# The shared expert's down product of a vision block, computed straight into rows of tokens instead of columns

## The chip, the cores and the metric

The kernel runs on one core of one Trainium2 chip. The metric is the device time of one execution in microseconds (us). A time is given as the median of several executions; a profile is one execution more, with its own time.

## The reference, cut to what matters

64 images give 38 tokens each (36 patches and two class tokens), 2432 tokens of 256 channels. One block follows: a gated linear attention on the normalised tokens, then a mixture of 32 experts with a shared expert. The part that the change touches is the shared expert:

```python
def _swiglu(x, gw, uw, dw):
    return jax.nn.silu(x @ gw) * (x @ uw) @ dw
...
shared_out = _swiglu(x, shared_gate_w, shared_up_w, shared_down_w)
...
return (shared_out + routed_out).reshape(b, s, h)
```

Here x has 256 channels and the hidden layer 512. The result is added to the residual, and each token's row is then added to the output of the one expert that the router picked for it.

## The kernel before, in words

**Phase one, groups.** The images go through in G = 8 groups of 8 images, so GT = 304 tokens a group. A group passes four stages: embedding (e), front (f: first layer norm, up product, convolution), attention (a), and mixture (m: second layer norm, router, shared expert). In each step of the program four different groups stand in the four stages. What follows what on each engine is written out by hand in one function `step` for each engine; semaphores with counts tie the engines together. The last three groups, called `near` (group 5), `next_last` (group 6) and `last` (group 7), leave the pipeline in three blocks that are written out in full behind the loop, with fewer stages in each.

**Layouts.** Products that contract over channels want channels on the partitions ("columns": 128 channels by 304 tokens). Layer norms, residual and stores want tokens on the partitions ("rows": three tiles of 114, 114 and 76 tokens, which `height(j)` and `columns(j)` give, with 256 channels). `to_rows` turns columns into rows by transposes on TensorE.

**The shared expert of a group.** For each of four chunks k of 128 hidden channels `gate_up(m, k)` makes gate and up in the banks mb[0] and mb[1]; ScalarE makes `silu_g` of the first, VectorE multiplies it with the second into `act_t[:, k, :]` (128 hidden channels by 304 tokens). `shared_down` then makes the product in columns: a 128x128 piece of the weights `sd_w` lies still, the 304 columns of `act_t` move. ScalarE copies both halves from the banks to `ffn_t`, six transposes of `ffn_rows` bring them back to the banks as rows, and `base_of` on VectorE adds the residual `h2` and writes `base_rows`, which SyncE stores and GpSimd scatters to the expert's zone in memory.

A product of f32 operands is executed as two passes, each with its own load of the weights: the 8 matmuls of 304 columns are 16 passes in the trace. Transposes are one pass each.

**Around it.** In a step of the pipeline TensorE runs `gate_up(m, 3)`, `up(f, 7)`, `shared_down(m)`, `embed(e, 0)`, `ffn_rows(m)`, `heads_t(a)`, `embed(e, 1)`, `down(a)`. `embed(e, 0)` waits until `silu_z` of the front stage has been read out of its bank. In the written-out blocks `shared_down` comes in two halves, placed between other work. `stream` is a matmul whose result nobody reads.

**Phase two, experts.** 37 slots of 128 tokens each (32 and five more for overfull experts). Each slot loads its expert's weights (1.5 MB), its token rows `xg` from the zones, and computes the expert; TensorE passes straight from the last `ffn_rows` to the transposes of the first slot's `xg`, ScalarE makes `x_hi` and VectorE `x_lo` of them, on which the first product waits.

Of the kernel before, what the change touches and what calls it, by code (L numbers as in the profile page):

```python
# [13 lines left out]
D = 256  # L14
# [9 lines left out]
GT = GS * S  # L24
# [21 lines left out]
def height(j):  # L46

    return SHORT if j == NT - 1 else R
# [10 lines left out]
def groups_phase(nc, block, patches, w_lin, pos, cols, w_up, conv, chan, wq, wk, wv, wvt, w_gates, b_gates,  # L59
# [6 lines left out]
    with ExitStack() as ctx:  # L66
        def sb(name, shape, dt=f32):
            return ctx.enter_context(nc.sbuf_tensor(name, shape, dt))

        def sem(name):  # L70
            return ctx.enter_context(nc.semaphore(name))
# [91 lines left out]
        act_t = sb("act_t", [128, KI, GT])  # L163
        ffn_t = sb("ffn_t", [128, KD, GT])
        base_rows = sort.base_rows
# [127 lines left out]
        s_act = sem("s_act")  # L293
        s_sd_mm = sem("s_sd_mm")
        s_ffn = sem("s_ffn")
        s_ft_mm = sem("s_ft_mm")
# [197 lines left out]
        def _(act):  # L494
# [9 lines left out]
            def copy(dst, src):  # L504
                return act.activation(dst, src, ACT.Copy)  # L505
# [140 lines left out]

            def ffn_t_of(m, halves=range(KD)):
                for c in halves:
                    act.wait_ge(s_sd_mm, KD * m.n + c + 1)
                    copy(ffn_t[:, c, :], mb[c][:, 0:GT]).then_inc(s_ffn, 1)  # L650

            def step(e, f, a, m):
# [43 lines left out]
                if f and f.n == 1:  # L696
                    x_act_of(f, 0)
                    x_act_of(f, 1)
                if m: ffn_t_of(m)
                if a: att_t_of(a)  # L700
# [40 lines left out]
            x_act_of(f, 1)  # L741
            ffn_t_of(m, (0,))

# [10 lines left out]
            v_of(a, 2)  # L754
            ffn_t_of(near, (1,))
            decay(a, 0)
# [11 lines left out]
            score_rows(m)  # L768
            ffn_t_of(m, (0,))
            att_t_of(a, (0,))  # L770
            ffn_t_of(m, (1,))

            def last_group(split):
                m = last
                xn2_t_of(m)
                split(0, 0)
                tanh_score(m)
                silu_g_of(m, 0)
                score_rows(m)
                silu_g_of(m, 1)  # L780
                split(0, 1)
                silu_g_of(m, 2)
                split(1, 0)
                silu_g_of(m, 3)
                split(1, 1)
                ffn_t_of(m)

# [519 lines left out]
        def _(pe):  # L1307
# [259 lines left out]

            def shared_down(m, halves=range(KD)):
                pe.wait_ge(s_act, KI * m.n + KI)
                for c in halves:  # L1570
                    for k in range(KI):
                        last = pe.matmul(mb[c][:, 0:GT], sd_w[:, k, c * 128:(c + 1) * 128], act_t[:, k, :],  # L1572
                                         start=(k == 0), stop=(k == KI - 1))
                    last.then_inc(s_sd_mm, 1)

            def ffn_rows(m):
                pe.wait_ge(s_ffn, KD * m.n + KD)
                to_rows(mb, ffn_t, s_ft_mm)

            def step(e, f, a, m):  # L1580
# [46 lines left out]
                if f: up(f, 7)  # L1627
                if m: shared_down(m)
                if e: embed(e, 0)
                if m: ffn_rows(m)  # L1630
                if a: heads_t(a)
# [48 lines left out]
            att_rows(a)  # L1680
            shared_down(m, (0,))

# [5 lines left out]
            v_of(a, 0)  # L1688
            shared_down(near, (1,))
            v_of(a, 1)  # L1690
# [3 lines left out]
            gates_t(a)  # L1694
            ffn_rows(near)
            tops_t(a)
# [13 lines left out]
            heads_t(a)  # L1710
            shared_down(m, (0,))
            down(a)
            att_rows(a)
            shared_down(m, (1,))
            ffn_rows(m)

# [11 lines left out]
            gate_up(m, 3)  # L1728
            shared_down(m)
            sort.slot_table(pe)  # L1730
            ffn_rows(m)

# [640 lines left out]
```

## Time and profile before

| | before |
|---|---|
| median of 3 runs | 653.28 us (651.33 to 653.66) |
| the profiled execution | 654.7 us |
| its span, first to last instruction | 652.9 us |
| mean granted TensorE clock | 0.988 of full |
| TensorE busy | 607.6 us, 93% |
| VectorE busy | 429.5 us, 66% |
| ScalarE busy | 375.2 us, 57% |

The span is what the trace shows; the time holds 1.8 us more for start and end. In the views an instruction's row begins with its start from the beginning of the span. "PE" is TensorE's matmuls, "PEld" its loads of weights, which overlap them, "DVE" VectorE, "ACT" ScalarE, "POOL" GpSimd and "SPq" the queue of SyncE. A matmul's duration holds its way through the array, so it is longer than the distance to the next one; what a pass costs in a row of passes is that distance.

### The profile page before, as it was taken

Reading aid. Unit: us, or ns where it says so; the run is one execution under the profiler, and the core shown is the slowest. Engines: PE = TensorE matmul, PEld = TensorE weight load, DVE = VectorE, ACT = ScalarE, POOL = GpSimd, SP = SyncE. Lnnn points to the kernel's source line nnn. Section 1 sums busy time; section 2 is a strip of 40 time slices with the busy share of each in tenths; the row PEclk is TensorE's granted clock in tenths of the full one; section 3 lists DMA queues with packets and bytes.
Section 4 is the critical chain, followed back from the end, with each engine's and each line's share of the span. In section 5 each row is a group of like instructions: output and inputs, shape, how many; then the busy total and the mean of one; then the engine's idle time right before and its main releaser. Section 6 shows DMA issues by size and latency. Waiting matters only on the chain.

```text
span 652.9 us, 10636 instructions
## 1 busy us (share of the span) xinstructions
PE 607.6 (93%) x3615; PEld 510.1 (78%) x3615; DVE 429.5 (66%) x1338; ACT 375.2 (57%) x839; POOL 197.4 (30%) x226
## 2 busy tenths in 40 slices
PE   4899899999998998999999998988999999999995
PEld 3688778878878878878878977766788888888884
DVE  1644785865856865866765866675876777776672
ACT  1328668449439529539538758243666666666661
POOL 5100110231232133133033233353256662232451
PEclk9999899999999999999998999899999999999999
DMA  8339410030030030030010011185999999999960
GB/s 291 132 85 369 122 56 1 20 94 21 20 95 21 20 94 21 19 95 21 8 51 20 2 37 37 35 303 169 392 391 378 379 348 350 373 369 404 343 214 23
DMA packets 44597, 101.56 MB, mean 156 GB/s; under 512 B 9295, under 2 KB 30589, under 8 KB 39672
## 3 DMA queue, kind: packets, MB, share of 16 engines
q1 hardware_dynamic: 35280, 89.07, 38.1%
q0 software_dynamic: 7696, 8.49, 4.7%
q10 hardware_dynamic: 1560, 3.23, 1.5%
q8 instruction: 32, 0.52, 0.4%
q14 instruction: 29, 0.24, 0.1%
HBM read 80.17 MB, written 23.32 MB: 159 GB/s over the span
## 4 chain that ended last, share of the span: by engine, by line
PE 71%; ACT 14%; DVE 8%; issue 2%; POOL 1%; DMA 1%; SPq 0%; DVEq 0%; ACTq 0%; POOLq 0%
PE bank L2253 16%; PE bank L1390 11%; PE bank L2272 9%; PE bank L1355 8%; PE bank L1512 4%; PE bank L1490 3%; PE bank L1455 3%; PE bank L2261 2%; PE bank L1416 2%; PE bank L1572 2%; PE bank L1364 2%; ACT v L505 2%; ACT hst L581 2%; ACT L596 1%; ACT L592 1%
## 5 line engine op out<-in xcount | busy, mean ns | idle before, releaser
L456 POOL TENSOR_TENSOR rstd_h<-var_h,minus_half 114x4 f32<-114x4 f32 (+1 forms) x24 | 24.3, 1014 | 173.3 <-DVE var_h L999 173.3
L2077 POOL DMA_INDIRECT out<-rows,bg x32 | 37.6, 1175 | 82.4 <-DVE rows L2143 81.1
L1355 PE MATMUL bank<-patch,lin_w 128*128 128x288 f32 x192 | 52.6, 428 | 8.7 <-DMA col_t<-cols 7.9
L2253 PE MATMUL bank<-w_hi,x_hi 128*128 128x512 f32 x148 | 56.5, 463 | 2.7 <-DVE x_lo L2155 2.7
L1355 PEld LDWEIGHTS bank<-patch,lin_w 128*128 128x128 f32 x192 | 37.4, 201 | 20.6 <-DMA col_t<-cols 7.9
L898 DVE SCALAR_TENSOR_TENSOR y<-xm,conv_t,y 128x296 f32<-128x296 f32 (+2 forms) x96 | 43.7, 512 | 6.2 <-ACT xm L505 6.2
L2253 PE MATMUL bank<-w_lo,x_hi 128*128 128x512 f32 x148 | 46.3, 394 | 0.0
L2253 PE MATMUL bank<-w_hi,x_lo 128*128 128x512 f32 x148 | 46.2, 393 | 0.0
L2179 DVE TENSOR_TENSOR act_e<-silu_e,bank 128x512 f32<-128x512 f32 x37 | 25.5, 688 | 31.0 <-PE bank L2253 30.3
L2149 DVE TENSOR_TENSOR w_lo<-wts,w_hi 128x1024 fp32r<-128x1024 f32 x36 | 43.1, 1217 | 0.5 <-ACT w_hi L2201 0.5
L2228 ACT ACTIVATE silu_e<-bank 128x512 f32<-128x512 f32 x37 | 22.1, 598 | 35.2 <-PE bank L2253 35.2
L1390 PE MATMUL bank<-xn_hi,up_hi 128*128 128x304 f32 x128 | 33.7, 346 | 6.0 <-ACT xm L505 4.9
L1841 POOL DMA_INDIRECT b_zone_dram<-base_rows,spot x24 | 31.1, 1295 | 26.9 <-DVE base_rows L1125 20.9
L505 ACT ACTIVATE att_t<-bank 128x304 f32<-128x304 f32 x15 | 6.3, 423 | 54.1 <-PE bank L1512 53.4
L2201 ACT ACTIVATE w_hi<-wts 128x1024 fp32r<-128x1024 f32 x36 | 36.8, 1049 | 0.0
L1841 POOL DMA_INDIRECT x_zone_dram<-xs_rows,spot x24 | 30.2, 1259 | 21.1 <-DVE spot L1103 9.0
L2196 ACT ACTIVATE x_hi<-bank 128x256 fp32r<-128x256 f32 x37 | 14.2, 383 | 38.9 <-PE bank L2242 28.1
L2143 DVE SCALAR_TENSOR_TENSOR rows<-bank,bg 128x256 f32<-128x256 f32 x37 | 15.7, 424 | 31.2 <-PE bank L2272 19.3
L1572 PE MATMUL bank<-act_t,sd_w 128*128 128x304 f32 x128 | 35.0, 424 | 1.2 <-DVE act_t L1117 1.2
L1390 PE MATMUL bank<-xn_hi,sgu_hi 128*128 128x304 f32 x128 | 31.6, 329 | 3.4 <-DVE act_t L1117 2.9
L1512 PE MATMUL bank<-hst,down_w 128*128 128x304 f32 x128 | 34.1, 420 | 0.1
L2272 PE MATMUL bank<-wts_down,act_et 128*128 128x256 f32 x144 | 34.1, 379 | 0.0
(261 smaller groups left out, 1658.8 us busy)
## 6 DMA issues: line engine op xcount, KB each, us to landing
wts<-w_exp SPq DMA_DIRECT2D x18, 1024.0 KB
x_act<-w_exp SPq DMA_DIRECT2D x10, 1024.0 KB
silu_z<-w_exp SPq DMA_DIRECT2D x9, 1024.0 KB
wts_down<-w_exp SPq DMA_DIRECT2D x18, 512.0 KB
patch<-patches SPq DMA_DIRECT2D x8, 864.0 KB, 6.0
down_w<-w_exp SPq DMA_DIRECT2D x10, 512.0 KB
lin_w<-w_exp SPq DMA_DIRECT2D x9, 512.0 KB
b_zone_dram<-act_t SPq DMA_DIRECT2D x1, 4160.0 KB, 28.4
```

Source lines behind the costliest of these rows:

```text
L898: dve.scalar_tensor_tensor(y[:, k, :, lag:], xm[:, f.p, k, :, 0:S - lag], w, y[:, k, :, lag:], ALU.mult, ALU.add).then_inc(s_conv, 1)
L1355: last = pe.matmul(fb[c][:, 0:GS * N], lin_w[:, k, c * 128:(c + 1) * 128], patch[:, k, :], start=(k == 0), stop=(k == KF - 1))
L1390: last = pe.matmul(dst, weights[w][:, c, at:at + 128], x[part][:, c, :], start=(n == 0), stop=(n == 3 * KD - 1))
L1512: last = pe.matmul(ab[c][:, 0:GT], down_w[:, k, c * 128:(c + 1) * 128], hst[:, k, :], start=(k == 0), stop=(k == KI - 1))
L1572: last = pe.matmul(mb[c][:, 0:GT], sd_w[:, k, c * 128:(c + 1) * 128], act_t[:, k, :], start=(k == 0), stop=(k == KI - 1))
L1841: pool.indirect_dma_start(zone, bass.IndirectOffsetOnAxis(ap=self.spot[0:n, t:t + 1], axis=0), rows[0:n, j, :], None, bounds_check=E * SLO ...
L2077: pool.indirect_dma_start(out, bass.IndirectOffsetOnAxis(ap=rows_at, axis=0), rows[:, k % 4, :], None, bounds_check=T - 1, oob_is_err=Fals ...
L2149: dve.tensor_tensor(w_lo[:, k % 2, u, :], wts[k % 4][:, u * KD * I:(u + 1) * KD * I], w_hi[:, k % 2, u, :].bitcast(f32), ALU.subtract).the ...
L2179: dve.tensor_tensor(act_e[:, e, :], silu_e[:, e, :], banks[3 + 2 * e][:, :], ALU.mult).then_inc(s_ae, 1)
L2201: act.activation(w_hi[:, k % 2, u, :], wts[k % 4][:, u * KD * I:(u + 1) * KD * I], ACT.Copy).then_inc(s_w_hi, 1)
L2253: last = pe.matmul(banks[2 + 2 * e + u][:, :], x[:, e, c * SLOT:(c + 1) * SLOT], w[:, e, u, c * I:(c + 1) * I], start=(n == 0), stop=(n == ...
L2272: last = pe.matmul(banks[6 + k % 2][:, 0:D], act_et[:, k % 2, c, :], wts_down[k % 4][:, c * D:(c + 1) * D], start=(c == 0), stop=(c == KI ...
```

## The change

The product is turned round. A tile of tokens of `act_t` (128 hidden channels by 114 or 76 tokens) lies still, and the 256 columns of `sd_w[:, k, :]` move. The result has tokens on the partitions, so `base_of` reads it from the banks as it is. `ffn_t`, the two copies of ScalarE and the six transposes are gone. Tiles 0 and 1 go to the two halves of mb[0], tile 2 to mb[1]. The first three products of tile 0 wait only for their own chunk of `act_t`, all others for the last one.

```diff
-        ffn_t = sb("ffn_t", [128, KD, GT])
...
-            def ffn_t_of(m, halves=range(KD)):
-                for c in halves:
-                    act.wait_ge(s_sd_mm, KD * m.n + c + 1)
-                    copy(ffn_t[:, c, :], mb[c][:, 0:GT]).then_inc(s_ffn, 1)
...
-            def shared_down(m, halves=range(KD)):
-                pe.wait_ge(s_act, KI * m.n + KI)
-                for c in halves:
+            def ffn_rows(m, tiles=range(NT)):
+                pe.wait_ge(s_sg, KI * m.n + KI)
+                for j in tiles:
                     for k in range(KI):
-                        last = pe.matmul(mb[c][:, 0:GT], sd_w[:, k, c * 128:(c + 1) * 128], act_t[:, k, :],
-                                         start=(k == 0), stop=(k == KI - 1))
-                    last.then_inc(s_sd_mm, 1)
-
-            def ffn_rows(m):
-                pe.wait_ge(s_ffn, KD * m.n + KD)
-                to_rows(mb, ffn_t, s_ft_mm)
+                        pe.wait_ge(s_act, KI * m.n + (k + 1 if j == 0 and k < KI - 1 else KI))
+                        last = pe.matmul(mb[j // 2][0:height(j), (j % 2) * D:(j % 2 + 1) * D], act_t[:, k, columns(j)],
+                                         sd_w[:, k, :], start=(k == 0), stop=(k == KI - 1))
+                    if j > 0:
+                        last.then_inc(s_ft_mm, 1)
...
                 if f: up(f, 7)
-                if m: shared_down(m)
+                if m: ffn_rows(m)
                 if e: embed(e, 0)
-                if m: ffn_rows(m)
                 if a: heads_t(a)
...
             att_rows(a)
-            shared_down(m, (0,))
+            ffn_rows(m, (0, 1))
...
             v_of(a, 0)
-            shared_down(near, (1,))
+            ffn_rows(near, (2,))
             v_of(a, 1)
...
             gates_t(a)
-            ffn_rows(near)
             tops_t(a)
...
             heads_t(a)
-            shared_down(m, (0,))
+            ffn_rows(m, (0, 1))
             down(a)
             att_rows(a)
-            shared_down(m, (1,))
-            ffn_rows(m)
+            ffn_rows(m, (2,))
...
             gate_up(m, 3)
-            shared_down(m)
+            ffn_rows(m)
             sort.slot_table(pe)
-            ffn_rows(m)
```

Three places of TensorE's order show what moved. A row counts matmuls as the program issues them (an f32 one is two passes), the shape is that of the result. First a step of the pipeline, from the last product of the front stage to the attention's down product. Before:

```order
622 L1390 MATMUL bank<-xn_lo,up_hi 128x304 x2
623 L1572 MATMUL bank<-act_t,sd_w 128x304 x8
624 L1355 MATMUL bank<-patch,lin_w 128x288 x6
625 L1364 MATMUL bank<-ident,ffn_t 114x128 x4
626 L1364 MATMUL bank<-ident,ffn_t 76x128 x2
627 L1501 MATMUL bank<-ident,o 128x114 x8
628 L1501 MATMUL bank<-ident,o 128x76 x4
```

And now:

```order
618 L1376 MATMUL bank<-xn_lo,up_hi 128x304 x2
619 L1559 MATMUL bank<-sd_w,act_t 114x256 x8
620 L1559 MATMUL bank<-sd_w,act_t 76x256 x4
621 L1341 MATMUL bank<-patch,lin_w 128x288 x6
622 L1487 MATMUL bank<-ident,o 128x114 x8
623 L1487 MATMUL bank<-ident,o 128x76 x4
```

Twelve matmuls of 256 columns stand ahead of the embedding where there were eight of 304, and nothing of the shared expert stands behind it any more. Second the block of group 6, where its shared expert meets the attention of group 7 (`o` is transposed by `heads_t`, `hst` read by `down`, `att_t` by `att_rows`; `ident` and `sd_w` with 128x512 is the filler). Before:

```order
789 L1501 MATMUL bank<-ident,o 128x114 x8
790 L1501 MATMUL bank<-ident,o 128x76 x4
791 L1572 MATMUL bank<-act_t,sd_w 128x304 x4
792 L1512 MATMUL bank<-hst,down_w 128x304 x8
793 L1364 MATMUL bank<-ident,att_t 114x128 x4
794 L1364 MATMUL bank<-ident,att_t 76x128 x2
795 L1572 MATMUL bank<-act_t,sd_w 128x304 x4
796 L1364 MATMUL bank<-ident,ffn_t 114x128 x4
797 L1364 MATMUL bank<-ident,ffn_t 76x128 x2
798 L1347 MATMUL bank<-sd_w,ident 128x512
799 L1381 MATMUL bank<-ident,xn 128x114 x2
```

And now:

```order
782 L1487 MATMUL bank<-ident,o 128x114 x8
783 L1487 MATMUL bank<-ident,o 128x76 x4
784 L1559 MATMUL bank<-sd_w,act_t 114x256 x8
785 L1498 MATMUL bank<-hst,down_w 128x304 x8
786 L1350 MATMUL bank<-ident,att_t 114x128 x4
787 L1350 MATMUL bank<-ident,att_t 76x128 x2
788 L1559 MATMUL bank<-sd_w,act_t 76x256 x4
789 L1333 MATMUL bank<-sd_w,ident 128x512
790 L1367 MATMUL bank<-ident,xn 128x114 x2
```

Ahead of the attention's down product four matmuls have become eight, behind it four matmuls and six transposes have become four matmuls. Third the end of phase one: the last group's shared expert, the small product of `slot_table` (from `slot_e`), and the first transposes and products of phase two. Before:

```order
838 L1390 MATMUL bank<-xn_lo,sgu_hi 128x304 x2
839 L1572 MATMUL bank<-act_t,sd_w 128x304 x8
840 L1910 MATMUL bank<-ident,slot_e 1x114
841 L1364 MATMUL bank<-ident,ffn_t 114x128 x4
842 L1364 MATMUL bank<-ident,ffn_t 76x128 x2
843 L2234 UNCONDITIONAL_BRANCH
844 L2242 MATMUL bank<-ident,xg 128x128 x2
```

And now:

```order
829 L1376 MATMUL bank<-xn_lo,sgu_hi 128x304 x2
830 L1559 MATMUL bank<-sd_w,act_t 114x256 x8
831 L1559 MATMUL bank<-sd_w,act_t 76x256 x4
832 L1890 MATMUL bank<-ident,slot_e 1x114
833 L2214 UNCONDITIONAL_BRANCH
834 L2222 MATMUL bank<-ident,xg 128x128 x2
```

The transposes between the slot table and the first slot are gone.

## Rows read from the trace of the kernel before

**Rows 1.** Page: busy us, share and instructions of the engines.

```profile
PE 607.6 (93%) x3615; PEld 510.1 (78%) x3615; DVE 429.5 (66%) x1338; ACT 375.2 (57%) x839; POOL 197.4 (30%) x226
```

**Rows 2.** Timeline of TensorE in one step of the pipeline: start, us, instruction, idle before.

```profile
222.54 4.32 PE L1572 MATMUL bank<-act_t,sd_w 128*128 128x304 f32 x16
227.02 3.15 PE L1355 MATMUL bank<-patch,lin_w 128*128 128x288 f32 x12 [0.16 <-ACT silu_z L544]
230.00 0.82 PE L1364 MATMUL bank<-ident,ffn_t 128*114 128x128 f32 x6
230.66 1.21 PE L1501 MATMUL bank<-ident,o 114*128 114x114 f32 x12
```

**Rows 3.** The chain that ended last: start, us, pieces of 304 and 256 columns.

```profile
234.83 4.09 PE bank L1512 x16
...
483.46 1.73 PE bank L2272 x8
```

**Rows 4.** Groups of instructions: busy us, mean ns of one, idle before.

```profile
L2272 PEld LDWEIGHTS bank<-wts_down,act_et 128*128 128x128 f32 x144 | 26.0, 190 | 2.9
```

**Rows 5.** Timeline of ScalarE in that step.

```profile
226.44 0.43 ACT L544 ACTIVATE silu_z<-bank 128x304 f32<-128x304 f32 x1
```

**Rows 6.** Timeline of TensorE between group 5's last products and group 7's decay.

```profile
380.72 0.82 PE L1364 MATMUL bank<-ident,att_t 128*114 128x128 f32 x6
382.10 2.31 PE L1572 MATMUL bank<-act_t,sd_w 128*128 128x304 f32 x8 [0.56 <-DVE act_t L1117]
384.25 2.21 PE L1416 MATMUL bank<-x_act,score_w 128*128 128x304 f32 x8
387.03 2.50 PE L1455 MATMUL bank<-q_t,x_act 128*114 128x122 f32 x24 [0.58 <-ACT q_t L566]
...
394.60 0.28 PE L1461 MATMUL bank<-logf,tri 114*114 114x12 f32 x2
```

**Rows 7.** Timeline of VectorE there.

```profile
394.15 0.17 DVE L924 SCALAR_TENSOR_TENSOR logf<-gl,fln 114x12 f32<-114x12 f32 x1 [2.38 <-ACT fln L596]
```

**Rows 8.** Timelines of TensorE, VectorE and GpSimd in group 6's block.

```profile
415.17 2.25 PE L1572 MATMUL bank<-act_t,sd_w 128*128 128x304 f32 x8
417.48 4.33 PE L1512 MATMUL bank<-hst,down_w 128*128 128x304 f32 x16
422.38 0.87 PE L1364 MATMUL bank<-ident,att_t 128*114 128x128 f32 x6 [0.57 <-DVE att_t L1029]
...
425.70 0.89 POOL L450 TENSOR_TENSOR rstd<-rstd,minus_half 114x3 f32<-114x3 f32 x1
...
426.60 1.02 DVE L1125 TENSOR_TENSOR base_rows<-bank,h 114x512 f32<-114x512 f32 x2 [1.31 <-PE bank L1364]
427.54 1.06 DVE L1054 TENSOR_SCALAR xn<-h,mv,rstd 114x256 f32<-114x256 f32 x3
```

**Rows 9.** Timeline of all engines where phase two begins.

```profile
441.22 4.36 PE L1572 MATMUL bank<-act_t,sd_w 128*128 128x304 f32 x16 [0.64 <-DVE act_t L1117]
...
444.14 0.82 SPq L2006 DMA_DIRECT2D xg<-x_zone_dram  x2
...
446.80 0.38 PE L2242 MATMUL bank<-ident,xg 128*128 128x128 f32 x2
446.88 1.02 DVE L1125 TENSOR_TENSOR base_rows<-bank,h 114x512 f32<-114x512 f32 x2 [1.82 <-PE bank L1364]
447.22 0.38 ACT L2196 ACTIVATE x_hi<-bank 128x256 fp32r<-128x256 f32 x1 [1.18 <-PE bank L2242]
...
447.96 0.40 DVE L2155 TENSOR_TENSOR x_lo<-bank,x_hi 128x256 fp32r<-128x256 f32 x1
448.42 0.73 PE L2253 MATMUL bank<-w_hi,x_hi 128*128 128x512 f32 x2 [1.24 <-DVE x_lo L2155]
```

**Rows 10.** Sums by stretch: us, busy of the engines, granted clock, DMA.

```profile
404.50:407.90 3.40, 1.24 (x10) 0.98 (x8) 3.19 (x23) 0.89 (x4) 1.33 (x2) 1.00 0.01 4
...
407.97:411.30 3.33, 3.33 (x15) 3.29 (x16) 2.76 (x19) 1.63 (x6) 1.37 (x2) 0.50 0.02 5
```

More of the change, by code:

```diff
@@ L293, in groups_phase @@
         s_act = sem("s_act")
-        s_sd_mm = sem("s_sd_mm")
-        s_ffn = sem("s_ffn")
         s_ft_mm = sem("s_ft_mm")
@@ L698, in step @@
                     x_act_of(f, 1)
-                if m: ffn_t_of(m)
                 if a: att_t_of(a)
@@ L741, in _ @@
             x_act_of(f, 1)
-            ffn_t_of(m, (0,))
             a, m = last, next_last
@@ L754, in _ @@
             v_of(a, 2)
-            ffn_t_of(near, (1,))
             decay(a, 0)
@@ L768, in _ @@
             score_rows(m)
-            ffn_t_of(m, (0,))
             att_t_of(a, (0,))
-            ffn_t_of(m, (1,))
             def last_group(split):
@@ L785, in last_group @@
                 split(1, 1)
-                ffn_t_of(m)
             sort.last_act = last_group
```

## The prediction, made before the changed kernel ran

> **What bounds the kernel now.** I read the page first: TensorE is busy for 93% of the span, no other engine above 66% [rows 1]. So an edit counts by what it does to TensorE's sequence of work, and by the few places where TensorE waits. The timeline of TensorE shows those. In the five steps of the pipeline in which the shared expert of groups 0 to 4 runs, the product, the embedding's first half, the six transposes of `ffn_t` and the head transposes follow each other with one short wait, for `silu_z` on ScalarE [rows 2]. In the written-out blocks of groups 5, 6 and 7 fewer stages run beside each other, and waits decide more [rows 6, 8, 9]. Behind the last group TensorE starts the experts at once, and the first product there waits for a chain over ScalarE and VectorE [rows 9].
>
> **The price of a pass.** In the chain 16 passes of 304 columns take 4.09 us and 8 passes of 256 columns take 1.73 us [rows 3]: 0.256 and 0.216 us a pass. Six transposes take 0.66 us, the distance from 230.00 to 230.66 in [rows 2], while their row lasts 0.82 us: a row's modelled end outlasts its turn by 0.16 us. I use that below: work that waited could have started by the shown idle time plus 0.16 us earlier.
>
> The new product has the stationary operand 114 or 76 wide, which no row shows together with 256 columns. Its bounds are the two prices above: 0.216 as in the experts' down product, which also moves 256 columns of f32 weights past stationary activations, and at most the 0.256 of the wider passes. I take 0.216, since columns and operands are the same. The load of weights takes 0.190 us there [rows 4], under the 0.216 of the pass beside it, and shows no cost.
>
> One rule of the Trainium skill speaks against this (TensorE: Matmul & The Clock Gate, Part 3, The mechanism): a load of weights overlaps running matmuls only where it addresses other row groups of the array. All loads here address the same ones. By it each pass would pay for its load; by [rows 3, 4] it does not, for 8 passes with 8 loads of 0.190 us took 1.73 us in all. The sum goes by the rows.
>
> **The work itself.** Removed for a group: 16 passes (16 x 0.256 = 4.10) and 6 transposes (0.66), 4.76 us of TensorE. Added: 12 matmuls, 24 passes, 24 x 0.216 = 5.18 us. TensorE does 0.42 us more for each group, 8 x 0.42 = 3.4 us in all. ScalarE loses two copies a group and VectorE nothing. The question is how much of the 3.4 us comes back out of waits.
>
> **Groups 0 to 4, in the pipeline: +0.04 us each, +0.2.** The product starts at 222.54, the embedding at 227.02 instead of 226.70 (idle 0.16 and 0.16), because `silu_z` ends at 226.87 [rows 2, 5]. From 222.54 to the head transposes at 230.66 are 8.12 us. Now: 5.18 for the passes and 0.06 to get going end at 227.78, behind `silu_z`, so nothing waits; the embedding needs 12 passes, 230.00 - 227.02 = 2.98 with a restart or 2.92 without; the head transposes start at 230.70. The wait has paid for the longer product. If that cover were gone, each step would cost 0.36. The copies taken from ScalarE and the earlier `base_rows` on VectorE free no one there: the steps behind wait for TensorE's own results.
>
> **Group 5: +0.4.** The first half waited for the last chunk of `act_t`: started at 382.10, could have at 382.10 - 0.56 - 0.16 = 381.38 [rows 6]. Now the first three products of tile 0 need only the earlier chunks, 6 passes, 1.3 us, and cover the wait. 16 passes end at 381.38 + 0.06 + 3.46 = 384.9, where `q_of` started at 384.25: 0.6 later, and ScalarE's copies of q, for which the scores wait 0.58 us, move along. Tile 2 then takes 8 x 0.216 = 1.73 instead of 8 x 0.256 = 2.05, 0.3 back, of which what counts is where TensorE meets the forget gates: `logf` was ready at 394.32 and its sum started at 394.60 [rows 6, 7]. With `logf` 0.6 later, 394.92 plus some hundredths, the sum starts at about 395.0: +0.4. The transposes that are gone behind it stood in time in which TensorE waited for the scan of the gates on VectorE, so their 0.66 us return nothing.
>
> **Group 6: +0.25.** Two tiles (3.46 and 0.06) stand ahead of `down` where 8 passes did: it starts at 415.17 + 3.52 = 418.7 instead of 417.48, 1.2 later, and so does everything up to `att_rows` (422.38) and the second layer norm's statistics of group 7. SyncE's first loads of expert weights move by the same; their first reader is ScalarE behind its copy of group 7's second norm, which stands further down this same chain, so nothing new waits for them. But before, VectorE stood with `base_rows` (426.60 to 427.62) between the statistics and `xn`, just after the 1/std was ready at 425.70 + 0.89 = 426.59 [rows 8]. Tile 2 now starts behind `att_rows`, at 422.38 + 1.15 + 0.71 = 424.25, is done at 426.0, and VectorE does `base_rows` while GpSimd makes the 1/std, which is ready at about 427.75. `xn` starts at 427.8 instead of 427.54. So 1.2 us late becomes 0.25.
>
> **Group 7: -1.0.** Here the product waited 0.64 us for `act_t` and could have started at 441.22 - 0.64 - 0.16 = 440.42 [rows 9]. Three products of tile 0 cover that wait again: 440.42 + 0.06 + 5.18 = 445.66, the slot table is two short passes, 0.2 like two transposes, so the first transposes of `xg` could run at 445.9 instead of 446.80. Their rows were asked for at 444.14 and were there by 446.8; when exactly, no row says. I take 446.2. Then VectorE: before, `base_rows` and the table held it to 447.96 although `x_hi` was ready at 447.22 + 0.38 = 447.60; now `base_rows` is nearly done by then. `x_lo` starts about 0.75 us behind the transposes, at 446.95, the first expert product at 447.4 instead of 448.42: -1.0. Bounds: transposes at 445.9 give -1.35, at 446.7 they give -0.4.
>
> **Sum.** 0.2 + 0.4 + 0.25 - 1.0 = -0.15 us. The profiled execution took 654.7 us, 1.4 above the median of the runs; the difference applies to both. 653.28 - 0.15 = **653.1 us**. Phase two is unchanged: a slot every 5.3 us on TensorE. A measurement of this kernel tells a change of about 0.5%, 3.3 us, from none.
>
> **Rivals.**
> - The work shows in full: no wait gives anything back, because the operands of tile 0 or `silu_z` come later than I read. All 3.4 us of added passes stay: 656.7. It is slower than before by the 0.5% bound only if practically nothing is returned, or if a pass costs more than 0.216: 192 new passes at 0.256 add 7.7 us to my sum, 660.8. It decides from 0.234 us a pass (3.4 / 192 = 0.018 over). For it: the operand's width has no row. Against: 0.256 belongs to more columns. Chance 0.08.
> - Loads of weights are not hidden behind passes of 256 columns. The mechanism in this kernel: each of the 192 passes pays its load of 0.190 [rows 4] as well, +36 us, 690. This is what the rule named above would do here. Against it stand the same 8 passes in 1.73 us [rows 3]. Chance 0.01.
> - The clock. After a stretch in which TensorE was busy for 1.24 of 3.40 us the clock was granted at half for 3.3 us (0.50, that is 1.2 GHz), which costs about 1.65 us [rows 10]. Group 6's block now has a pause of about 1.2 us ahead of the transposes of `xn`, for the transposes of `ffn_t` are gone and the filler runs earlier; and every other wait shifts a little. One such stretch more: 654.8. Chance 0.14. One less, since the last blocks have moved: 651.5. Chance 0.13.
> - Group 6's delay is not returned, because VectorE's `base_rows` still stands before `xn` (tile 2 late): 654.1. Chance 0.08.
> - The change helps more: the earlier start of phase two and ScalarE's free time take more than 3.3 us out. For it I find no wait of that size behind the places changed. Chance 0.04.
>
> **How the numbers follow.** My forecast has the remaining 0.52, with its own range of 652.3 to 653.9 from the bounds of group 7 and the spread of the terms. Slower by over 0.5%: the first two rivals, 0.09. Faster by over 0.5%: the last rival, and 0.01 for two clock stretches less, 0.05. Within 0.5%: the rest, 0.86. The median before itself came from runs 2.3 us apart, so the range takes in one clock stretch either way: 651.2 to 655.4.
>
> **What would show each step.** A distance of 0.216 us between the new passes; from the start of the product to the head transposes about 8.16 us in the pipeline, without a wait ahead of the embedding; in group 5 the scores 0.6 us later relative to `att_rows`; in group 6 `down` 3.5 us behind the product's start and `base_rows` ahead of the ready 1/std; in group 7 no idle time before the product and some 7.0 us from its start to the first expert product (7.2 before, and from a start that was 0.8 later). I would be wrong if passes are dearer, if the many waits on `act_t`, one for each matmul, hold up the loads of weights, or if half-clock stretches come or go.

## The result, and the profile after

| | before | after |
|---|---|---|
| median, both kernels on the same chips | 653.28 us (13 runs) | 656.81 us (13 runs) |
| ratio, 95% interval | | 1.0062 [1.0038, 1.0086] |
| the profiled execution | 654.7 us | 660.08 us |
| its span | 652.9 us | 658.3 us |
| mean granted clock | 0.988 | 0.979 |

The change makes the kernel 3.5 us slower. The forecast was 653.1 us, no change. One execution far above the rest (699.68 us, of e3 below) and one of the kernel before (3382.77 us, beside e1 to e4) are left out of the ratios. The page of after, busy us and share of each engine (against [rows 1]):

```profile
PE 614.0 (93%) x3631; PEld 518.0 (79%) x3631; DVE 429.6 (65%) x1338; ACT 370.0 (56%) x823; POOL 197.6 (30%) x226
```

TensorE is busy for 6.4 us more, of which the added passes explain 3.4. The timeline of TensorE in the step of [rows 2]:

```profile
222.83 5.34 PE L1559 MATMUL bank<-sd_w,act_t 128*114 128x256 f32 x24
228.01 3.07 PE L1341 MATMUL bank<-patch,lin_w 128*128 128x288 f32 x12
230.92 1.21 PE L1487 MATMUL bank<-ident,o 114*128 114x114 f32 x12
```

The 24 passes take 228.01 - 222.83 = 5.18 us, 0.216 each, no wait stands ahead of the embedding, and from the product to the head transposes it is 8.09 us where it was 8.12. The same holds from step to step: from group 0's product (start at 121.76 us, before 121.45) to group 4's (323.90, before 323.66) it is 202.14 us, before 202.21. The pipeline costs nothing.

Group 5's block, TensorE from `att_rows` on (against [rows 6]):

```profile
384.15 0.82 PE L1350 MATMUL bank<-ident,att_t 128*114 128x128 f32 x6
384.81 3.62 PE L1559 MATMUL bank<-sd_w,act_t 128*114 128x256 f32 x16
388.26 2.21 PE L1402 MATMUL bank<-x_act,score_w 128*128 128x304 f32 x8
...
398.38 0.37 PE L1447 MATMUL bank<-logf,tri 114*114 114x12 f32 x2
399.26 0.28 PE L1453 MATMUL bank<-ident,a_gate 114*114 114x114 f32 x1 [0.51 <-DVE fsum L919]
400.23 0.31 PE L1457 MATMUL bank<-ident,top_gate 114*114 114x114 f32 x1 [0.69 <-DVE top_gate L924]
400.79 0.40 PE L1465 MATMUL bank<-mask_bf,ident_bf 114*114 114x456 bf16 x1 [0.24 <-DVE top_parts L930]
...
404.86 2.06 PE L1333 MATMUL bank<-sd_w,ident 128*128 128x512 f32 x2
406.71 1.06 PE L1476 MATMUL bank<-v,cw 114*114 114x128 f32 x4
```

The block is reached 3.4 us later than before, since the clock was at half from 353.9 us on for longer; that differs from execution to execution in both kernels (below). Inside the block, `att_rows` to `logf`'s sum is 14.23 us, before 13.88. At the gates TensorE now waits 0.51, 0.69 and 0.24 us. Before, the six transposes of `ffn_t` stood in between, and it waited 0.51 and 0.38:

```profile
395.39 0.29 PE L1467 MATMUL bank<-ident,a_gate 114*114 114x114 f32 x1 [0.51 <-DVE fsum L933]
396.06 0.87 PE L1364 MATMUL bank<-ident,ffn_t 128*114 128x128 f32 x6 [0.38 <-ACT ffn_t L505]
396.76 0.26 PE L1471 MATMUL bank<-ident,top_gate 114*114 114x114 f32 x1
396.92 0.40 PE L1479 MATMUL bank<-mask_bf,ident_bf 114*114 114x456 bf16 x1
```

And the filler (L1333) takes 2.06 us instead of 1.1. The windows say why. A row gives the stretch and its length, then the busy time (and the number of instructions) of TensorE, its loads, VectorE, ScalarE and GpSimd, then TensorE's granted clock and the DMA's share and GB/s:

```profile
395.00:398.20 3.20, 3.20 (x28) 2.89 (x26) 0.82 (x4) 3.14 (x6) 0.00 (x0) 1.00 0.00 0
398.20:401.60 3.40, 1.96 (x14) 1.35 (x13) 2.84 (x12) 2.81 (x6) 0.00 (x0) 1.00 0.01 2
401.70:408.50 6.80, 6.80 (x33) 5.74 (x32) 3.93 (x19) 5.35 (x19) 3.51 (x3) 0.50 0.31 89
```

TensorE was busy for 1.96 of 3.40 us at the gates, and then the clock was granted at 0.50, 1.2 GHz, for 6.8 us. In the kernel before the same place had 1.00:

```profile
394.70:398.00 3.30, 2.41 (x21) 2.01 (x19) 2.81 (x11) 2.88 (x7) 0.00 (x0) 1.00 0.00 0
398.00:401.40 3.40, 3.40 (x31) 2.91 (x30) 2.72 (x15) 3.36 (x16) 2.24 (x2) 1.00 0.26 73
```

These stretches aren't cut at the same instructions. Cut alike, as the 3.40 us from 14.05 us behind the start of `att_rows`, the busy time of TensorE at the gates is 1.96 us in after and was 2.51 before. The profile of before has its own 3.3 us at half clock further on, from 407.9 us [rows 10]; after has none there.

Group 6 (against [rows 8]) behaves as forecast: `down` stands 3.49 us behind the product, and `base_rows` lies ahead of the ready 1/std.

```profile
421.02 3.65 PE L1559 MATMUL bank<-sd_w,act_t 128*114 128x256 f32 x16
424.51 4.26 PE L1498 MATMUL bank<-hst,down_w 128*128 128x304 f32 x16
...
432.17 1.02 DVE L1111 TENSOR_TENSOR base_rows<-bank,h 114x512 f32<-114x512 f32 x2
...
432.65 0.89 POOL L447 TENSOR_TENSOR rstd<-rstd,minus_half 114x3 f32<-114x3 f32 x1
...
433.57 1.05 DVE L1040 TENSOR_SCALAR xn<-h,mv,rstd 114x256 f32<-114x256 f32 x3 [0.39 <-POOL rstd L447]
```

Group 7 (against [rows 9]), all engines:

```profile
446.16 1.45 POOL L1821 DMA_INDIRECT x_zone_dram<-xs_rows,spot  x1 [0.30 <-issue]
...
451.08 0.82 SPq L1986 DMA_DIRECT2D xg<-x_zone_dram  x2
...
453.11 0.44 PE L2222 MATMUL bank<-ident,xg 128*128 128x128 f32 x2 [1.02 <-DMA xg<-x_zone_dram]
...
454.48 0.73 PE L2233 MATMUL bank<-w_hi,x_hi 128*128 128x512 f32 x2 [0.93 <-DVE x_lo L2135]
```

TensorE is free at 452.1 and waits 1.02 us for the rows of `xg`. SyncE asked for them 4.92 us behind the start of the last scatter into the zone; before it was 444.14 - 440.13 = 4.01, with this scatter:

```profile
440.13 1.45 POOL L1841 DMA_INDIRECT x_zone_dram<-xs_rows,spot  x1 [0.30 <-issue]
```

### The profile page after: what moved, and what is told of

It is laid out like the page before. It is cut to its first block, busy times and chain, and to the rows that moved or that the text cites. A ratio compares the mean times of both kernels' runs of the same rounds, so it can differ in the third digit from the quotient of the medians.

```text
span 658.3 us, 10662 instructions
## 1 busy us (share of the span) xinstructions
PE 614.0 (93%) x3631; PEld 518.0 (79%) x3631; DVE 429.6 (65%) x1338; ACT 370.0 (56%) x823; POOL 197.6 (30%) x226
## 4 chain that ended last, share of the span: by engine, by line
PE 76%; ACT 12%; DVE 7%; issue 2%; POOL 1%; DMA 1%; SPq 0%; DVEq 0%; POOLq 0%
PE bank L2233 16%; PE bank L1376 12%; PE bank L2252 9%; PE bank L1341 8%; PE bank L1559 5%; PE bank L1498 5%; PE bank L1476 3%; PE bank L1441 3%; PE bank L2241 2%; PE bank L1402 2%; ACT hst L578 2%; ACT v L502 1%; PE bank L1350 1%; PE bank L1487 1%; PE bank L1413 1%
## 5 line engine op out<-in xcount | busy, mean ns | idle before, releaser
L1559 PE MATMUL bank<-sd_w,act_t 128*114 128x256 f32 (+1 forms) x192 | 43.1, 379 | 0.0
L1559 PEld LDWEIGHTS bank<-sd_w,act_t 128*114 128x114 f32 (+1 forms) x192 | 31.7, 168 | 8.2
```

The source lines that it names most:

```text
L1559: last = pe.matmul(mb[j // 2][0:height(j), (j % 2) * D:(j % 2 + 1) * D], act_t[:, k, columns(j)], sd_w[:, k, :], start=(k == 0), stop=(k = ...
```

## The experiments

Ratios are to the kernel before on the same chip, with 95% intervals, of 12 or 13 executions of each kernel and 23 to 35 of before. A "stretch" is time at half clock in the profiled execution; "at the gates" is the place at 401.7 us in after. Stretches elsewhere differ from profile to profile of one and the same kernel. Both kernels have one at about 353 us in most profiles (3.4 or 10.2 us, sometimes none), and mostly short ones at 33 and 74 us. One of 3.4 us at about 408 us is in the profiles of before, e5 and e9, and not in those of e1 and e3. Short ones where phase two begins are told of at the end. The table of landmarks further down begins behind the stretches at 33, 74 and 353 us. One profile shows one execution; so the mean granted clock, which every execution has, is compared as well.

**1. Which part.** Both kernels again, the new product in groups 0 to 4 alone, and in groups 5 to 7 alone. The line of e3 (in e4 the pipeline keeps the old lines and the three blocks have the new ones):

```diff
                 if f: up(f, 7)
-                if m: shared_down(m)
+                if m: ffn_direct(m)
                 if e: embed(e, 0)
-                if m: ffn_rows(m)
                 if a: heads_t(a)
```

> The kernel before, unchanged, as a control and for the granted clock of every run. Two theories of the 3.5 us are at stake. Clock theory: the new passes cost what was forecast and waits return them, but TensorE is granted the half clock for longer in the blocks written out behind the pipeline. Then here runs at a lower mean clock are the longer ones, by about half of the time at half clock: 0.001 of mean clock is worth about 0.65 us, and the mean clock lies near 0.988. Work theory: the 3.4 us of added passes stay in the time whatever the clock does; then before and after differ at equal clock.

> The changed kernel, unchanged, on the same chip. Clock theory: about 3.5 us slower in the median, at a mean clock lower by about 0.005, and equal to before at equal clock to within 1 us; the profile's stretches at half clock add up to more than those of before, around 353 and 401 us. Work theory: slower by 3.4 us also at equal clock.

> The new product only in the five steps of the pipeline (groups 0 to 4); groups 5, 6 and 7 keep columns, copies and transposes. Clock theory: same as before to within 0.5 us, for the steps of the pipeline measured 0.03 us shorter each in the trace of the change and have no half clock. Work theory: 5 x 0.42 = 2.1 us slower.

> The new product only in the written-out blocks of groups 5, 6 and 7; the pipeline is as before. Clock theory: all of the loss is here, 3 to 4 us slower than before, with a mean clock as low as that of the change. Work theory: 3 x 0.42 = 1.3 us slower.

| | median us | ratio | stretch at the gates |
|---|---|---|---|
| e1 before again | 650.12 | 0.9979 [0.9956, 1.0002] | none |
| e2 after again | 654.82 | 1.0063 [1.0033, 1.0093] | 6.8 us |
| e3 groups 0 to 4 | 652.62 | 1.0024 [0.9996, 1.0052] | none |
| e4 groups 5 to 7 | 654.98 | 1.0053 [1.0023, 1.0083] | 6.8 us |

The loss repeats and comes with the written-out blocks. The theory that the added work simply stays wanted 2.1 us in e3 and 1.3 in e4; the ratios give 1.6 and 3.5 us. The profile of e4, its slowest execution (661.3 us), has a second stretch, behind the wait of 1.26 us ahead of group 6's `xn`:

```profile
432.60:436.00 3.40, 2.08 (x8) 0.90 (x8) 2.18 (x7) 0.74 (x2) 2.79 (x3) 1.00 0.89 360
436.10:442.80 6.70, 6.10 (x29) 5.96 (x30) 2.19 (x18) 2.88 (x6) 1.37 (x2) 0.50 1.03 380
```

That is the place that the prediction feared. It came in one of the eight profiles with that order there (after, e2, e4, e5, e6, e13, e16, e18).

**2. Which group, or a filler.** e5 keeps columns in group 5; e6 and e7 are the changed kernel with fillers, e8 is the kernel before with its transposes moved.

```diff
             gates_t(a)
+            pe.wait_ge(s_v, NT * a.n + 1)
+            stream(ab[0], sd_w, 1)
             tops_t(a)
...
             m = last
-            stream(ab[1], sd_w, 1)
+            stream(ab[1], sd_w, 2)
```

The last two lines are in e7 only. e8:

```diff
             gates_t(a)
-            ffn_rows(near)
             tops_t(a)
+            ffn_rows(near)
```

> The changed kernel with group 5 alone left in columns, with its copies and its six transposes between the gates' transpose and the tops' transpose. Theory gates: the transposes stood in a wait of TensorE (it now idles 0.69 and 0.24 us there) and kept the activity of that stretch up; without them the clock is halved for 6.8 us from about 401 us. Then this kernel has no 6.8 us stretch there and loses at most 1 to 2 us to before. Rival, the pause of 1.25 us in group 6's block or the experts' start costs it: then it is as slow as the change, 3.5 us.

> The changed kernel with one dummy matmul of 512 columns (two passes, 0.86 us, result unread) in the wait ahead of the tops' transpose in group 5's block; more work, nothing shared with the product itself. Theory gates: no half clock from 401 us, about 2 to 3 us faster than the change, although TensorE does 0.86 us more. Rival theories (the work of the passes, or the pause in group 6's block): same as the change or up to 0.2 us slower.

> As the last, and the filler ahead of the transposes of xn of group 7 doubled, which covers most of the pause of 1.25 us in group 6's block. If that pause also halves the clock in some executions (one profile of the kernel with the change in the blocks alone had a stretch at 436 us), this is faster by up to 1 us than the filler at the gates alone; if not, the same.

> The kernel before with one edit: group 5's six transposes stand behind the tops' transpose instead of ahead of it, so TensorE idles in the wait for the scan, as in the changed kernel. The decay starts 0.4 us later at most. Theory gates: the half clock comes from about 400 us on and this kernel is 2 to 3.5 us slower than before, at a lower mean clock, without any new product. Rivals: at most 0.4 us slower.

| | median us | ratio | stretch at the gates |
|---|---|---|---|
| e5 group 5 in columns | 654.11 | 1.0028 [1.0003, 1.0053] | none |
| e6 filler at the gates | 653.12 | 1.0016 [1.0000, 1.0031] | none |
| e7 and ahead of `xn` | 652.76 | 1.0022 [0.9998, 1.0046] | none |
| e8 before, moved | 651.64 | 1.0007 [0.9984, 1.0030] | none |

More work on TensorE made the kernel faster: e6 does 0.87 us more than after, and its ratio is 1.0016 where after's is 1.0062 and e2's 1.0063, with intervals that don't meet. e7's second filler adds nothing that can be measured. e8 missed its forecast of 2 to 3.5 us: the transposes stand behind `top_gate`'s wait there, and no stretch follows, so to have the wait uncovered isn't enough. e5 has no stretch at the gates and is still 1.8 us slower than before, by an interval that just excludes 1; its profile has three others, at 354, 408 and 449 us. What is left there, and why, is open.

**3. A better version?** e9 spreads the new product's tiles (in group 5 behind `att_rows`, behind the first v and behind `gates_t`; in group 6 tile 0 ahead of `down`, 1 and 2 behind `att_rows`), leaves out the filler ahead of group 7's `xn` and moves VectorE's `base_rows` behind `xn_lo`. e10 is the kernel before without its filler behind `decay`. e11 is e9, e12 the kernel before, each with a filler at 351 us:

```diff
+            pe.wait_ge(s_v, NT * a.n + 1)
+            stream(ab[0], sd_w, 1)
             f_sums(a)
             gates_t(a)
             up(f, 0)
```

> The changed kernel with the tiles of the product placed otherwise in two blocks: group 5's tile 0 ahead of q, tile 1 behind the first values, tile 2 in the wait behind the gates' transpose; group 6's tile 0 ahead of the attention's down product, tiles 1 and 2 behind its rows, in place of the filler, with VectorE's base_rows behind xn_lo of group 7. Amount theory (what counts for the clock is how much TensorE does in the stretch around the gates, and placement costs what the sum says): no half clock at 400 us; the decay of group 7 0.6 us earlier than before, the transposes of xn 0.9 us earlier; 1.5 to 2 us faster than before, 4 to 5 faster than the change. Rival, the new product itself lowers the clock wherever it stands: still 2 us or more slower than before.

> The kernel before with one edit: without the dummy matmul of 512 columns behind group 7's decay, in a stretch in which TensorE then waits for the weighted scores. It takes 0.86 us of TensorE's activity out of the same stretch from which the change took 0.66 us of transposes. Amount theory: half clock from 401 us in most executions, as in the change, 2 to 3 us slower than before. Rival, the clock follows the new product or its place and not the amount: same as before within 0.5 us.

> As the spread kernel, with one dummy matmul of 512 columns ahead of the sum of the forget gates in group 6's attention, about 351 us, in the 0.36 us wait there (it also delays that sum by up to 0.4 us). At about 353.5 us the clock falls in both kernels, for 3.4 us in some profiles and 10.2 us in others. If the amount of activity decides, it falls less often here: 1 to 2 us faster than the spread kernel in the median, and without executions at 655 us and over.

> The kernel before with the same filler at 351 us and nothing else. Amount theory: 1 to 2 us faster than before in the median, for the same reason. It tells whether a gain of the last kernel belongs to the change or could be had without it.

e9: 652.26 us, 1.0017 [0.9987, 1.0047]. e10: 651.85, 1.0005 [0.9979, 1.0032], and no stretch at the gates. e11: 650.44, 0.9970 [0.9941, 0.9998]. e12: 649.82, 0.9963 [0.9939, 0.9987]. The gain of e11 is that of the filler, for e12 has it without the change. e9 missed its forecast of 1.5 to 2 us faster than before. On the path the spread tiles do gain: the first expert product comes 65.20 us behind `att_rows` in e11, 66.43 in e12. But e11's profile has a 3.4 us stretch where phase two begins, and from that product to the end it takes 204.7 us, e12 202.7.

e10 missed its forecast too, and it doesn't test what it was meant to. In before, the filler that it leaves out starts at 399.48 us, 18.8 us behind `att_rows`; in after the clock falls about 17.5 us behind them, ahead of that filler. In the 3.40 us at the gates TensorE is busy for 2.51 us in e10, as in before; it is the next 3.40 us that have 3.06 instead of 3.40. A stretch of 3.4 us comes later in e10's profile, at 412.4 us.

In e12 the place where both kernels mostly ran at half clock reads

```profile
350.00:360.20 10.20, 9.31 (x77) 8.36 (x78) 6.74 (x31) 9.76 (x27) 2.89 (x2) 1.00 0.12 32
```

against this row of after:

```profile
353.95:364.10 10.15, 10.15 (x51) 9.98 (x51) 4.79 (x23) 7.31 (x20) 0.00 (x0) 0.50 0.01 4
```

**4. The six transposes themselves.** e13 is the changed kernel with six transposes that nobody reads, at their old place:

```diff
             gates_t(a)
+            pe.wait_ge(s_v, NT * a.n + 1)
+            for j in range(NT):
+                for c in range(KD):
+                    pe.transpose(ab[0][0:height(j), c * 128:(c + 1) * 128], sd_w[:, c, 0:height(j)], ident[:])
             tops_t(a)
```

e14 is the kernel before with the new product in group 5 alone, e15 the same for group 7 alone:

```diff
-            shared_down(m)
+            ffn_direct(m)
             sort.slot_table(pe)
-            ffn_rows(m)
```

e16 is the changed kernel with the fillers of e6 and of e12.

> The changed kernel with six transposes that nobody reads (0.66 us of TensorE) at the place where group 5's transposes were. If the six transposes kept TensorE active enough there: no stretch at half clock near 401 us, granted clock in the medians up from 0.983-0.987 to about 0.990, ratio to before 1.001 to 1.003. If only more work than that (the filler's 0.8 us) does it, or if what they were waiting for mattered: the stretch stays and the ratio stays 1.006.

> The kernel before with the new product in group 5 alone. If group 5's missing transposes bring the half clock near 401 us: a stretch of about 6.8 us there, ratio 1.004 to 1.006, nearly the whole loss. If the stretch needs the other groups too: no such stretch, 1.000 to 1.001 from the 0.4 us of longer product.

> The kernel before with the new product in group 7 alone. By the prediction: first expert product 1.0 us earlier counted from the start of the product's wait, ratio 0.9985. By the reading of the trace (rows of xg land about 2 us after SyncE asks for them, and TensorE waits for them): from group 7's gate products to the first expert product -0.2 to +0.5 us, ratio 1.000 to 1.001, no clock stretch at 401 us.

> The changed kernel with both fillers, at the gates of group 5's block and at 351 us. If the loss is the half clock plus about 1 us of longer order: clock 0.993 to 0.997, about 651 us, ratio to before 0.998, some 1 us above the kernel before with its filler (649.8, 0.9963). If the product itself still costs its 3.4 us: 653, 1.002. If it costs nothing at an even clock: 649.8.

| | median us | lowest us | ratio |
|---|---|---|---|
| e13 dead transposes | 652.82 | 650.68 | 1.0018 [0.9992, 1.0045] |
| e14 group 5 alone | 654.38 | 653.03 | 1.0063 [1.0032, 1.0094] |
| e15 group 7 alone | 652.16 | 649.29 | 0.9993 [0.9959, 1.0027] |
| e16 two fillers | 653.03 | 650.84 | 1.0006 [0.9983, 1.0029] |

e14 changes nothing but group 5 and has the whole loss; e13 leaves the change as it is, adds work without use, and takes most of the loss away. The intervals of the two ratios overlap a little, and e13's profile happens to have no stretch at all, not at 33, 74 or 353 us either, so the profile alone wouldn't do. The clock of the single executions settles it: of the 49 executions of after, e2, e4 and e14 none has a mean granted clock above 0.992; e13 has four of 12 at 0.995 to 0.999, e6 four of 12 at 0.995 to 0.997, and of the 128 of the kernel before beside e1 to e18, 44 lie above 0.992, the highest at 0.998. e16 missed its 651 us by 2: with both fillers the change is as fast as before, no faster. TensorE at the gates in e14:

```profile
393.58 0.28 PE L1465 MATMUL bank<-ident,a_gate 114*114 114x114 f32 x1 [0.51 <-DVE fsum L931]
394.55 0.31 PE L1469 MATMUL bank<-ident,top_gate 114*114 114x114 f32 x1 [0.69 <-DVE top_gate L936]
395.10 0.40 PE L1477 MATMUL bank<-mask_bf,ident_bf 114*114 114x456 bf16 x1 [0.25 <-DVE top_parts L942]
```

and in e13:

```profile
393.24 0.28 PE L1453 MATMUL bank<-ident,a_gate 114*114 114x114 f32 x1 [0.51 <-DVE fsum L919]
393.36 0.82 PE L1681 MATMUL bank<-ident,sd_w 128*114 128x128 f32 x6
394.21 0.31 PE L1457 MATMUL bank<-ident,top_gate 114*114 114x114 f32 x1
394.77 0.40 PE L1465 MATMUL bank<-mask_bf,ident_bf 114*114 114x456 bf16 x1 [0.24 <-DVE top_parts L930]
```

`a_gate` to the first `mask_bf` is 1.52 us in e14 and 1.53 in e13; before it was 396.92 - 395.39 = 1.53. The dead transposes cost no time on the path and fill the pause. The windows of e14:

```profile
392.80:396.40 3.60, 2.16 (x16) 1.70 (x17) 2.97 (x11) 3.01 (x8) 0.00 (x0) 1.00 0.00 0
396.55:403.30 6.75, 6.75 (x31) 5.69 (x31) 3.61 (x19) 5.62 (x17) 3.52 (x3) 0.50 0.31 90
```

and of e13:

```profile
392.00:395.40 3.40, 2.62 (x22) 1.94 (x19) 2.70 (x11) 2.97 (x6) 0.00 (x0) 1.00 0.01 2
395.50:402.00 6.50, 6.50 (x56) 5.99 (x55) 5.42 (x30) 6.37 (x20) 3.65 (x3) 1.00 0.32 90
```

Cut alike, as the 3.40 us from 14.05 us behind the start of `att_rows`, TensorE is busy at the gates for 1.96 us in after, e4 and e14, 1.97 in e2 and 2.62 in e13. So the amount and the clock go together in these; what in the work counts, and how much of it is needed, the runs don't tell.

**5. Group 7's missing microsecond.** e17 is e15 with e12's filler, e18 has the new product in group 6 as well.

```diff
-            shared_down(m, (0,))
+            ffn_direct(m, (0, 1))
             down(a)
             att_rows(a)
-            shared_down(m, (1,))
-            ffn_rows(m)
+            ffn_direct(m, (2,))
```

> The kernel before with the new product in group 7 alone and the filler at 351 us. If group 7's 0.8 us and the filler's 2.5 us add up: about 649.0, ratio 0.995, clock 0.993 or more, 17.3 us from group 7's router to the first expert product. If group 7's part is lost again once the filler is there: 649.8, 0.996, 18.1 us.

> The same with the new product in group 6 as well. If group 6's earlier rows bring the late landing of group 7's scatter: from the last scatter into x_zone_dram to SyncE's request for xg 4.7 to 5.3 us instead of 4.1, and 17.9 to 18.5 us from the router to the first expert product; ratio 0.996. If the late landing comes from the pipeline or from group 5: 4.1 us, 17.3 us, ratio 0.995. In both no half clock near 401 us, for group 5 keeps its transposes.

e17: 651.66 us, 0.9990 [0.9967, 1.0013]; it was meant to be the fastest version and isn't measurably so. e18: 652.71, 1.0017 [0.9996, 1.0037]. The traces are clearer. SyncE and GpSimd in e17, the last scatter and what follows it:

```profile
425.11 0.36 SPq L1833 DMA_DIRECT2D wts<-w_exp  x1
...
441.00 0.82 SPq L2016 DMA_DIRECT2D xg<-x_zone_dram  x2
```

```profile
436.80 1.45 POOL L1851 DMA_INDIRECT x_zone_dram<-xs_rows,spot  x1 [0.30 <-issue]
```

and in e18:

```profile
426.10 1.56 SPq L1830 DMA_DIRECT2D wts<-w_exp  x1
...
443.09 0.82 SPq L2013 DMA_DIRECT2D xg<-x_zone_dram  x2
```

```profile
438.18 1.45 POOL L1848 DMA_INDIRECT x_zone_dram<-xs_rows,spot  x1 [0.30 <-issue]
```

From scatter to request 4.20 us in e17 and 4.91 in e18. Group 6's new form is what delays it. Their times don't show group 7's gain, and hardly can: from the first expert product to the end, where the kernels are alike, the profiles without a stretch there differ by up to 1.9 us (202.6 in e14, 204.5 in before).

**The landmarks**, starts on TensorE read from the timelines, in us from the transposes of group 5's `att_rows`. The stretches at 33, 74 and 353 us lie ahead of them.

| start of | e1 before | after | e13 | e15 | e18 |
|---|---|---|---|---|---|
| `logf` sum | 13.88 | 14.23 | 14.23 | 13.88 | 13.87 |
| decay's first `v,cw` | 19.69 | 22.56 | 20.14 | 19.69 | 19.68 |
| `heads_t` of group 7 | 32.14 | 35.82 | 32.53 | 32.15 | 32.13 |
| router of group 7 | 48.35 | 52.22 | 48.93 | 48.37 | 48.53 |
| first `xg` transpose | 64.82 | 68.96 | 65.75 | 64.30 | 65.23 |
| first expert product | 66.44 | 70.33 | 67.12 | 65.67 | 66.60 |

## Why the prediction was wrong

**The price of a pass and the work itself: right.** 0.216 us a pass, with loads that cost nothing. Both rivals on it fall: the passes aren't dearer than 0.216, and 24 loads ahead of 24 passes took 5.18 us in all. The first rival's other half, that no wait gives anything back, named 656.7 us, and 656.81 was measured; that is a coincidence, for e6, e7, e13 and e16 do all the added work and more and lose 0.4 to 1.4 us.

**Groups 0 to 4: right.** Forecast +0.04 us a step, the trace has 8.09 for 8.12, -0.03, and -0.07 over four steps. e3's 1.0024 has an interval that holds 1; it shows no loss, and excludes none below 3.4 us.

**Group 5: +0.4 forecast, +0.35 at `logf`'s sum and +0.45 at the decay in e13.** The sum was right. The sentence behind it was not: "The transposes that are gone behind it stood in time in which TensorE waited for the scan of the gates on VectorE, so their 0.66 us return nothing." They return nothing on the path, as e14 and e13 agree to 0.01 us. But I costed their removal at nothing, and they were what kept TensorE active there. This is the step that failed. Removing them, with the product turned round ahead of them, brings 6.8 us at half clock: from `logf`'s sum to `heads_t` after has 35.82 - 14.23 = 21.59 us, e13 32.53 - 14.23 = 18.30, so 3.3 us. That is the size of the loss. The clock was a rival, at 0.14, but I looked for it in group 6, where I expected a pause of 1.2 us ahead of `xn`; that pause came (1.25 us in after) and was followed by a stretch in e4's profile alone. I also priced a stretch by [rows 10] at 1.65 us, as 3.3 us long, and this one was twice as long. The stretch of [rows 10] itself comes and goes: e1, the same kernel again, has none there. The three short waits at the gates, 0.51, 0.69 and 0.24 us, each looked harmless in a view sorted by wait.

The Trainium skill (TensorE: Matmul & The Clock Gate, Part 4, PE-mode transpose) says that a transpose does not count as activity for the clock in the way a matmul does. Taken by that, e13 should have kept the stretch. The trace does not agree: with six dead transposes, 0.82 us in their row, the granted clock stayed at 1.00 behind the gates, as it did with the filler of e6, an ordinary matmul, and four executions of each reach a mean clock of 0.995 or more.

**Group 6: +0.25 forecast, +0.15 measured.** e13 is behind e1 by 20.14 - 19.69 = 0.45 us at the decay and by 48.93 - 48.35 = 0.58 at group 7's router; e18, with group 5 in columns, by 0.18. `down` was 3.49 us behind the product (forecast 3.52), and `base_rows` was ahead of the 1/std.

**Group 7: -1.0 forecast, nothing measured.** From the router to the first expert product e1 takes 18.09 us, e15 17.30: the mechanism gives -0.8 when it stands alone, inside the bounds I gave. In the whole change e13 takes 18.19, after 18.11. I took the rows of `xg` to be asked for as before and to lie ready at 446.2. With the new form in group 6 SyncE can ask for `xg` only 4.7 to 5.5 us behind the start of group 7's last scatter (ten of the eleven traces; e4 has 3.6 behind its second stretch), not 4.0 to 4.3 (all nine with the old form). From the scatter to the request 0.57 MB moved in after (116 GB/s over 4.92 us) and 0.46 in e15 (113 over 4.08). That group 6's form does it is shown by e17 and e18. How, stays open. One candidate was SyncE's load of `wts`, which takes 1.56 us instead of 0.36 to hand over in e18; but in e9 and e11, with `base_rows` behind `xn_lo`, it takes 0.40 and 0.41, and the request still comes 4.73 and 5.17 us behind the scatter.

**The sum.** With group 7 at +0.1 and group 6 at +0.15 the forecast's terms give -0.15 + 0.4 + 0.15 + 0.1 = +0.5 us; the clock adds 3.3. Together 3.8, measured 3.5 (0.0062 of 653.28 is 4.05). Without the clock's part e6, e7, e13 and e16 lie 0.0006 to 0.0022 above the kernel before, 0.4 to 1.4 us, around those 0.5; so little can't be told from no change. e5, with 0.0028 or 1.8 us, lies above them and isn't explained by this sum.

## What to carry to other kernels

Work in the shadow of a wait can have a second use: here it kept TensorE's clock up. Before taking such work out, read TensorE's busy time in windows over that place and not only the single waits, and try the removal with dead work in its place. If that is faster, look at the granted clock of every execution, not of one profile. And give each group of a written-out end its own experiment: the path terms of this sum were right to 0.4 us alone, and the largest of them was undone by its neighbour's change.

## What was not expected of the hardware

- Waits of 0.51, 0.69 and 0.24 us, with TensorE busy for 1.96 of 3.40 us, were followed by 6.8 us at half clock in all four profiles with that order (after, e2, e4, e14). The lowest time of the 36 executions of e2, e4 and e14 is 653.03 us, while e13 reaches 650.68, and none of the 49 with after's has a mean clock above 0.992: it seems to come every time. In e8, with another order there, it did not come.
- A filler of 0.87 us at 351 us, read by nobody, made the kernel before 0.37% faster (e12). Its 12 executions lie within 1.6 us, where the 35 of the kernel before on the same chip lie 8.4 us apart. Much of that spread goes with the clock: the 14 of them with a mean of 0.993 or more took 649.2 to 651.1 us, the four at 0.985 or less 654.9 to 657.7.
- Phase two's start can lose the clock too. e18 waits there for `xg` and then reads

```profile
442.90:446.20 3.30, 1.65 (x9) 0.63 (x7) 1.64 (x7) 0.38 (x1) 1.15 (x1) 1.00 0.58 142
446.30:449.60 3.30, 3.12 (x7) 2.51 (x8) 0.12 (x1) 0.16 (x1) 2.23 (x2) 0.50 0.91 332
```

  e5, e6 and e11 have such a stretch as well: four of the eleven profiles with the new form in group 6, and none of the nine with the old one. From the first expert product to the end these four take 204.7 to 205.4 us, the others 202.6 to 204.5. Whether it explains e18's 1.0017 against e17's 0.9990, or what is left of e5's loss, was not tried.
